# First attention of a two-layer network: one program over head pairs and halves of the queries, instead of two programs over whole head pairs

## The reference, cut to what matters

```
xn = layernorm(x, ln_scale, ln_bias)          # x: (2, 1024, 128), itself a layernorm of the input
q, k, v = (xn @ w) as (2, 16 heads, 1024, 8)  # for wq, wk, wv
probs = softmax(q @ k.T / sqrt(128))          # (2, 16, 1024, 1024)
out = probs @ v, heads side by side, + xn
```

## Time and profile before

| what | us |
|---|---|
| median of 3 runs | 1138.79 (1138.75 to 1138.86) |
| profiled execution | 1138.22 |
| its span, first to last instruction | 1136.4 |
| PE busy | 1016.6 |
| DVE busy | 730.4 |
| ACT busy | 664.9 |
| POOL busy | 395.1 |

### The profile page before, as it was taken

The page is one execution under the profiler, slowest core; times in us unless marked ns, Lnnn a source line. Parts: engine busy times, 40 slices in busy tenths (PEclk is TensorE's granted clock), DMA queues, the critical chain, the costliest instruction groups (busy, mean ns, idle before and its releaser), DMA issues. The chain is left out here.

```text
span 1136.4 us, 17320 instructions
## 1 busy us (share of the span) xinstructions
PE 1016.6 (89%) x5320; PEld 550.2 (48%) x5320; DVE 730.4 (64%) x1231; ACT 664.9 (59%) x1419; POOL 395.1 (35%) x340
## 2 busy tenths in 40 slices
PE   4499999999999997679579999999999999589997
PEld 3123333333333321423457676767777676456665
DVE  5588888888888870622744545545455554678997
ACT  4037777777777776312255655555565554357887
POOL 5650000000000000000567657493765730256665
PEclk9579999999999999589789999999999999789999
DMA  4300000000000000100000000000000000000001
GB/s 161 114 3 16 16 23 21 14 14 14 21 21 14 14 2 0 26 1 0 14 1 10 1 1 5 10 1 6 10 1 1 6 1 1 12 8 19 14 18 44
DMA packets 21230, 19.32 MB, mean 17 GB/s; under 512 B 5300, under 2 KB 15516, under 8 KB 21172
## 3 DMA queue, kind: packets, MB, share of 16 engines
q1 hardware_dynamic: 19844, 14.92, 4.5%
q0 software_dynamic: 528, 2.10, 0.5%
q10 hardware_dynamic: 800, 1.57, 0.4%
HBM read 14.26 MB, written 4.19 MB: 16 GB/s over the span
## 5 line engine op out<-in xcount | busy, mean ns | idle before, releaser
L484 ACT ACTIVATE probs<-score_bank 128x512 f32<-128x512 f32 x512 | 277.7, 594 | 121.4 <-PE score_bank L538 120.1
L415 DVE TENSOR_REDUCE maxima<-max_bank 128x1 f32<-128x1024 f32 x256 | 301.7, 1220 | 57.2 <-PE max_bank L505 55.2
L538 PE MATMUL score_bank<-q_stack,k_stack 100*128 100x512 bf16 x512 | 164.4, 387 | 7.0 <-ACT probs L484 5.0
L1105 ACT ACTIVATE a_probs<-a_scores,a_lowest 128x896 f32<-128x896 f32 (+7 forms) x128 | 94.9, 741 | 112.7 <-DVE a_lowest L1100 112.1
L505 PE MATMUL max_bank<-k_stack,q_stack 96*128 96x512 bf16 x512 | 143.9, 401 | 17.5 <-PEq L164 12.0
L1350 PE MATMUL a_sum<-a_turned,a_v 128*128 128x512 f32 (+3 forms) x384 | 158.5, 500 | 0.8 <-ACT a_headsT L1279 0.6
L549 PE MATMUL summed<-probs,v_tile 128*32 128x512 f32 x1024 | 136.4, 605 | 1.0 <-ACT probs L484 1.0
L709 POOL MEMSET m_padded<- 128x96 f32 x1 | 0.2, 178 | 383.6 <-POOLq L361 383.6
L1100 DVE TENSOR_REDUCE a_lowest<-a_scores 128x1 f32<-128x896 f32 (+7 forms) x128 | 96.2, 756 | 40.8 <-PE a_scores L1094 40.3
L538 PEld LDWEIGHTS score_bank<-q_stack,k_stack 100*128 100x128 bf16 x512 | 44.1, 97 | 157.2 <-ACT probs L484 143.1
L1482 POOL TENSOR_TENSOR m_gated<-m_linear,m_sigm 128x512 f32<-128x512 f32 x64 | 87.8, 1372 | 46.5 <-ACT m_sigm L1577 46.5
(11 more groups left out here) (220 smaller groups left out, 1583.4 us busy)
## 6 DMA issues: line engine op xcount, KB each, us to landing
rope<-in_rope POOLq DMA_DIRECT2D x1, 2048.0 KB, 11.9
m_w<-in_L_ffn_mlp_w SPq DMA_DIRECT2D x32, 64.0 KB, 1.8
q_stack<-q_parts SPq DMA_DIRECT2D x32, 48.0 KB
k_stack<-k_parts SPq DMA_DIRECT2D x32, 48.0 KB
q_stack<-q_parts SPq DMA_DIRECT2D x32, 32.0 KB
k_stack<-k_parts SPq DMA_DIRECT2D x32, 32.0 KB
out<-x SPq DMA_DIRECT2D x4, 256.0 KB, 2.4
q_parts<-l_q_parts SPq DMA_DIRECT2D x1, 768.0 KB, 3.5
```

Of the source, the lines that this page charges most:

```text
L415: dve.reduce_max(maxima[:, (s + away) % 2, n:n + 1], max_bank[n % 2][:, :], AX_X).then_inc(max_ready, 1)
L484: act.activation(probs[:, k % PROB_STEPS, j, :], score_bank[j % 2][:, :], ACT.Exp, scale=SCALE0).then_inc(prob_ready, 1)
L538: pe.matmul(score_bank[j % 2][:, :], k_stack[s % STACKS][x][rows, k * P:(k + 1) * P], q_stack[s % STACKS][rows, half * CH:(half + 1) * CH] ...
L1105: act.activation(probs[:, k % 2, c, 0:row_width(n)], scores[n % 2][:, 0:row_width(n)], ACT.Exp, bias=lowest[:, n % 8:n % 8 + 1], accum_out ...
```

## The change

One function, `layer0`, replaces both programs, with no barrier between projection and attention. Its work is in 32 units, each a head pair with half of the queries (512). A unit has eight steps of 128 keys.

- **Scores** lie in two halves of the rows: the first head in rows 0 to 49, the second in rows 64 to 113, of one k stack and one q stack (48 rows of products, 2 rows for the maxima). Each score matmul names its half (`tile_position=(x * ROW, 0)`). There are three score banks instead of two. Two scores a step.
- **Searches** contract all 128 rows, against a k stack that holds one head alone (`k_alone`), zeros elsewhere. One search a step; eight per unit; 256 in all. 12 of them are made ahead of the first score.
- **Ring**: the two double banks are now shared in strict turn by searches, the turned maxima (`turn`, at step 4) and the folded heads (`fold`, at step 6). PE may fill place p only when DVE has freed place p - 2.
- **Use** takes two steps of keys at once: four matmuls in four column strips, at steps 1, 3, 5 and 7. The four strips of `summed` hold two heads x two keys' parities; `fold`, four f32 matmuls of 18 columns, turns them and adds the two parities. It replaces the four transposes; DVE divides 64 instead of 128 results per row at a time, twice as often.
- **Start**: x comes in two halves, each normalised by itself. The first pair's parts are sent by themselves to DRAM and loaded from there in six DMAs. Loads of a later pair are 18 DMAs instead of 12. `rope` (2 MB, for the second layer) is loaded by SP during unit 0 instead of by POOL at the start. POOL instead of DVE stages the values.

The diff, cut to its core:

```diff
+ROW = 64
+VW = 32
+UNITS0 = B * H0
+TILES = TB
+LEAD = TILES + 4
+FOLD_AT = 6
+RING = 2
+SCORES = 3
+PROBS = 4
+VALUE = HD0 + 1
+def ring_of_step(u, k):
+    m = TILES * u + k + LEAD
+    if m < TILES * UNITS0:
+        yield "search", m
+    if k == LEAD - TILES and u + 1 < UNITS0:
+        yield "turn", u + 1
+    if k == FOLD_AT and u >= 1:
+        yield "fold", u - 1
...
+                    for part in range(3):
+                        rows = slice(first, first + (3 - part) * HD0)
+                        first += (3 - part) * HD0
+                        sp.dma_start(q_stack[stack][rows, :],
+                                     t.parts_dram[0][part, head, :].unsqueeze(0).broadcast_to([3 - part, HD0, S])).then_inc(loaded[stack], 16)
+                        for keys in (k_alone[stack][x], k_stack[stack]):
+                            sp.dma_start(keys[rows, :], t.parts_dram[1][0:3 - part, head, :]).then_inc(loaded[stack], 16)
...
+                def subtract(u):
+                    pair, half = divmod(u, 2)
+                    sp.wait_ge(freed, PLACE["turn", u] + 1)
+                    for part in range(2):
+                        row = NST + part
+                        sp.dma_start(q_stack[pair % STACKS][row:row + ROW + 1:ROW, half * CH:(half + 1) * CH],
+                                     shift[:, u % 2, part, :]).then_inc(shift_in[u % 2], 16)
...
+                send_first(0)
+                send_first(1)
+                sp.wait_ge(first_out, 16 * 6)
+                load_first()
+                send_parts(0)
...
+                for x in range(2):
+                    load_head(1, x)
+                send_parts(1)
+                subtract(0)
+                for u in range(UNITS0):
+                    if u + 1 < UNITS0:
...
+                    pair, x = u // 2 + 2, u % 2
+                    if pair < NPAIR:
+                        if pair >= STACKS:
+                            sp.wait_ge(score_ready, (pair - STACKS + 1) * 2 * 2 * TB)
+                        if pair == NPAIR // B and x == 0:
+                            sp.wait_ge(parts_out[1], 16 * 2)
+                        load_head(pair, x)
+                    if u == 0:
+                        sp.dma_start(t.rope[:, :, :], d["rope"].rearrange("a p s -> p a s")).then_inc(rope_in, 16)
...
+                    queries = slice(side * CH + qt * P, side * CH + (qt + 1) * P)
+                    for half in range(2):
+                        last = pe.matmul(max_bank[place % RING][:, half, :], q_stack[stack][:, queries],
+                                         k_alone[stack][x][:, half * CH:(half + 1) * CH], start=True, stop=True)
...
+                    for c in range(4):
+                        last = pe.matmul(max_bank[place % RING][:, 0, c * 2 * VALUE:(c + 1) * 2 * VALUE], heads[u % 2][:, c * P:(c + 1) * P],
+                                         fold[:, :, :].rearrange("p x w -> p (x w)"), start=True, stop=True)
+                    last.then_inc(filled, 1)
...
+                def give_ring(use):
+                    what, n = use
+                    place = PLACE[use]
+                    if place >= RING:
+                        pe.wait_ge(freed, place - RING + 1)
...
+                def score(u, k, x):
+                    pair, half = divmod(u, 2)
+                    rows, e = slice(x * ROW, x * ROW + NST + 2), 2 * (u * TB + k) + x
...
+                    if e >= SCORES:
+                        pe.wait_ge(prob_ready, e - SCORES + 1)
+                    pe.matmul(score_bank[e % SCORES][:, :], k_stack[pair % STACKS][rows, k * P:(k + 1) * P],
+                              q_stack[pair % STACKS][rows, half * CH:(half + 1) * CH], start=True, stop=True,
+                              tile_position=(x * ROW, 0)).then_inc(score_ready, 1)
...
+                    for slot in range(4):
+                        k, x = 2 * g + slot // 2, slot % 2
+                        last = pe.matmul(summed[VW * slot:VW * (slot + 1), :], v_tile[pair % 2][:, x, k, :], probs[:, k % PROBS, x, :],
+                                         start=(g == 0), stop=(g == GROUPS - 1), tile_position=(0, VW * slot))
+                    last.then_inc(used, 1)
...
+                        for x in range(2):
+                            score(u, k, x)
+                        for event in ring_of_step(u, k):
+                            give_ring(event)
+                        if k == 1 and u >= 1:
+                            use(u - 1, GROUPS - 1)
+                        if k % 2 == 1 and k >= 3:
+                            use(u, (k - 3) // 2)
+                use(UNITS0 - 1, GROUPS - 1)
+                give_ring(("fold", UNITS0 - 1))
...
-                def body(g, s):
-                    for k in range(TB):
-                        tiles = [tile for tile in searched_at(k) if ahead(g, s, tile[0])]
-                        for j in range(2):
-                            score(g, s, k, j)
-                        if first(g, s) and k == 0:
-                            search(g, s, *tiles.pop(0))
-                        if k > 0:
-                            use(g, s, k - 1)
-                        elif not first(g, s):
-                            use(g, s - 1, TB - 1)
-                        if k == 2 and not first(g, s):
-                            turn_heads(g, s - 1)
-                        if k == TURN_AT and ahead(g, s, 1):
-                            turn_maxima(g, s + 1)
-                        for j in range(2, 4):
-                            score(g, s, k, j)
-                        for tile in tiles:
-                            search(g, s, *tile)
```

More of the change, by code:

```diff
@@ L30 @@
 NST = 6 * HD0
-SHIFTS = 2 * NST
-VW = 32
 H1, KV1, D1 = 8, 4, 128
@@ L115 @@
 STACKS = 4
[L118 to L129, removed]
@@ L308, in layer0_attention, with ring_before, ring_uses, layer0 @@
+def ring_before():
+    for m in range(LEAD):
+        yield "search", m
+        if m == TILES:
+            yield "turn", 0
+def ring_uses():
+    yield from ring_before()
+    for u in range(UNITS0):
+        for k in range(TB):
+            yield from ring_of_step(u, k)
+    yield "fold", UNITS0 - 1
+PLACE = {use: i for i, use in enumerate(ring_uses())}
+def layer0(nc, t, d):
     ctx = ExitStack()
@@ L350, in ahead, with loads_by @@
-        def ahead(g, s, n):
-            return not isinstance(g, int) or 4 * g + s + n < NPAIR
-        def first(g, s):
-            return isinstance(g, int) and 4 * g + s == 0
-        def searched_at(k):
-            return [divmod(MAX_LEAD + 2 * k + i, TILES) for i in range(2)]
+        heads_ready, inverse_ready = sem("heads_ready"), sem("inverse_ready")
+        NW = 8
+        CB = NCH // B
+        GROUPS = TB // 2
+        LOADS = [6] + [18] * (NPAIR - 1)
+        SET = 4 * STACKS
+        def loads_by(pair):
+            return 16 * sum(LOADS[p] for p in range(pair % STACKS, pair + 1, STACKS))
@@ new lines, in normalise_chunk, with take_rest @@
+                def normalise_chunk(c):
+                    for tile in range(4 * c, 4 * c + 4):
+                        last = dve.tensor_scalar(normed[:, tile, :], t.x[:, tile, :], moments.both[:, tile, 0:1],
+                                                 moments.inverse[:, tile:tile + 1], ALU.subtract, ALU.mult)
+                    last.then_inc(normed_ready, 1)
+                def take_rest(i):
+                    which, c, cols = unit(i)
+                    dve.wait_ge(hi_ready, i + 1)
+                    if i >= 4:
+                        dve.wait_ge(lo_ready, i - 3)
+                    dve.tensor_tensor(rest[:, i % 4, :], bank_of_unit(i), parts[which][:, 0, cols], ALU.subtract).then_inc(rest_ready, 1)
@@ new lines, in take_ring @@
+                def take_ring(use):
+                    what, n = use
+                    if what == "search":
+                        search(n, PLACE[use])
+                    if what == "turn":
+                        split(n, PLACE[use])
+                    if what == "fold":
+                        divide(n, PLACE[use])
+                find(0)
+                normalise_chunk(0)
+                normalise_chunk(1)
+                find(1)
+                take_rest(0)
+                take_rest(1)
@@ L491, in _ @@
+                take(UNITS0 - 1)
             @block.tensor
             def _(pe):
[L493 to L507 removed]
```

597 lines of the change are left out of this document (284 added, 313 removed).

## The result

| | before | changed |
|---|---|---|
| median of the runs, us | 1138.82 (4 runs) | 1177.14 (1173.26 to 1180.12, 4 runs) |
| span of the profiled execution, us | 1136.4 | 1176.0 |
| first score of the first attention | 69.27 | 58.00 |
| end of its last division | 454.87 | 493.83 |
| from there to the end | 681.5 | 682.2 |

The changed kernel is slower: ratio 1.0335, interval 1.0308 to 1.0363. The forecast was 1167 us, in a range of 1136 to 1190. The attention starts 11.3 us earlier and takes 50.2 us longer from first score to end (435.8 against 385.6); what lies behind it is the same within 0.7.

A forecast was written before the change was run, and what follows sets the result against it. PE, without gaps, bound the kernel before; afterwards the two-place ring would hold PE. 1138.2 - 17.8 (start) + 45.7 (attention, units of 13.45) = 1166.1, median 1167 us, range 1136 to 1190.

The forecast's parts named there:

- the ring: Two shared bank places: PE waits for DVE's maxima at steps 4 to 5 and 6 to 7, 1.86 us each.
- 1.85, 1.86, 1.86, 1.05 and 1.28: Us between search starts: odd to even steps (four times), 4 to 5, 6 to 7, 0 to 1, 2 to 3.
- The sum 13.45: One unit of the middle in us, all eight search intervals added; 1.5 more than half of an old pair.
- Halves overlap: A step's two scores, in different row halves, take the price of one: 0.22 us, other bound 0.44.
- changes of form cost 0.10: Each new change of PE's array division between scores, search and use group costs 0.10 us, bounds 0 and 0.2.
- Serial halves: Rival: row halves do not overlap, a score pair costs 0.44, a unit 14.1 us, total 1187; chance 0.16.
- free changes: Rival: changing the array's division costs nothing, a unit takes 12.45 us, total 1137, not slower; chance 0.15.
- changes of 0.2: Rival: each change costs 0.2 us, twelve or so per unit, 14.4 or more, total above 1190; chance 0.08.
- From first score to end: First attention, first score to last division: 431.3 us against 385.6 before, +45.7, with 2 for half clock at the start.
- The start: Time until the first score: 51.5 us (49 to 56) against 69.27 before, a gain of 17.8.
- The first search: Searches begin at 35 us against 41.68: 5 less with rope moved and x halved, six loads at 1.1 each.
- half a pair: Old kernel's 11.93 us, the mark for one new unit; rival: a unit costs no more, 1121 us or less, chance 0.11.

The follow-up runs named there:

- Experiment 1: Changed kernel with the turned maxima placed ahead of step 4's search instead of behind it, for PE and DVE: 1152.33 us.
- experiment 6: Changed kernel with turned maxima and fold each ahead of their step's search, and the first maxima sent earlier: 1141.28 us, ratio 1.0024 to the kernel before.
- experiment 7: Changed kernel plus strings of score halves, searches and use groups behind the first attention, alternating and each kind alone, waiting for nothing: 1261.73 us, one run.
- Experiment 4: Changed kernel with SP sending the first maxima ahead of the second head's loads and the second sequence's parts: 1169.04 us, 8.1 less than the changed kernel.
- experiment 9: Kernel before with one edit: the rope table loaded during the first attention instead of at the start: 1138.08 us, ratio 0.9991.
- experiment 2: Changed kernel with each score matmul over all 128 rows instead of row halves, leaving out the separation of heads: 1174.63 us, 2.5 less than the changed kernel.
- experiment 3: Changed kernel with the use group ahead of the search in odd steps and the turn ahead of step 5's search: 1167.94 us, ratio 1.0248 to the kernel before.

## Why the prediction was right, and where it was off

- **What decides** was named rightly: the ring. Experiment 1 shows it by 24.8 us, and experiment 6 by some 29 of the 50.2 us by which the attention is longer; the other 20 are the changes of form, the fold and ACT, which the sum had too. The intervals forecast as 1.85, 1.86, 1.86, 1.05 and 1.28 came as 1.85, 1.92, 1.93, 1.14 and 1.27. The sum 13.45 was short by 0.23, thirty times 0.23 is 6.9 us. The terms that were too small are the two waits for DVE's maximum (1.86 for 1.92 and 1.93) and the one for ACT's exponential (1.05 for 1.14). For a maximum the sum had 1.18, half of the row for two; one by itself ends after 1.23 (243.30), and 0.64 + 1.23 + 0.05 is the 1.92. Of the signs named, one did not come: PE is busy 91.7% of the middle and not below nine tenths.
- **Halves overlap, changes of form cost 0.10**: both as forecast, by experiment 7. Serial halves, free changes and changes of 0.2 are out. The rule in the Trainium skill's "TensorEngine Tiling (Array Packing)", Key Properties, that a change of mode drains TensorE, agrees with the 0.10 to 0.12 us that each change costs here. The Trainium skill's "TensorE: Matmul & The Clock Gate", Measured speedup vs the span model, has 3.07 times for four row tiles; the estimate of 0.25 for two halves that the prediction worked out from it is a little dear: they take 0.22.
- **From first score to end**: 431.3 forecast, 435.8 measured: 6.9 more in the units, 1.6 less at the beginning (the first unit, whose first five us run at half clock, is 0.4 longer than the others, where 2 was allowed for the clock), 0.8 less in the tail.
- **The start** is the larger miss: first score 58.00 for 51.5, outside my 49 to 56. The mis-sized terms stand in SP's stream. From the end of the first loads until the parts were sent and landed it took 7.6 (32.9 to 40.48) and not 4.5; the eighteen loads took 10.7 (until 51.2) and not 11.7; the parts held SP 2.4 for 0.8; and from the issue of the maxima to the first score it was 4.4 instead of the 2.7 of the earlier trace rows, behind 1.5 MB of parts. Experiment 4 takes the last two away and gives 8.1 us.
- **The first search** came at 36.70 for 35, and so near by luck in part. The last part left at 24.8 and not at 22, so the gain there was 2 us and not 5, and the six loads took 4.7 and not 6.6. The reason with rope was wrong: by experiment 9 its 2 MB held the weights up but not PE, which waited for DVE.
- Together: 6.5 for the start, 4.5 for the attention and 0.7 behind it on the sum of 1166.1 make 1177.8; the profiled execution took 1178.45, the median is 1177.14. Both errors go the same way, and the median lies 10 us above the 1167, just outside the 1153 to 1176 that the forecast had for itself, and inside the stated range.

**Where half a pair's time went.** In experiment 6, where DVE holds almost nothing up, a unit is four double steps of 2.72 (two pairs of halves 0.44, two searches 0.87, a use group 0.87, five changes 0.54), the fold 0.91 (250.80 to 251.72), the turn with its short wait 0.26, and 0.27 and 0.41 at steps 1 and 3, where a score's bank waits for ACT: 12.73, measured 12.72. Half a pair before is four steps of 2.88 and 0.4: 11.93. So the halves save 1.76 us a unit (eight pairs at 0.22), and three more changes in a double step take back 1.3 of it; some 0.2 of small waits in before's four steps are gone; fold and turn cost 0.8 more, ACT's banks 0.7. Together that is 0.8 more than half a pair. On top of it the changed kernel has 0.96 of waits for the ring. The split of the 0.8 is worked out from rows; no run took the fold or ACT's waits away by themselves.

## What to carry to other kernels

- Count how often TensorE changes its form in a loop before splitting its rows or columns. Two halves at the price of one save 0.22 here, and a pair that stands between two whole-row matmuls gives it all back in two changes (experiment 2). By the prices of experiment 7 it pays to gather matmuls of one form first; no run here did.
- In a ring of two that one engine fills in order and another frees, a short task given behind a long one makes the filler wait for the long one. Give the short task first: 0.8 us a unit here, for two lines. But look at where the work moves: experiment 3, which also gave the turn first, put three tasks between two searches and gained 9 us, not 25.
- Time a large change in parts: here a start by which, alone, the attention ends 5.7 us earlier was hidden under a middle that takes 50 us longer.

## What the runs showed of the hardware that I had not expected

TensorE stood at half clock behind two short waits. In experiment 7, at the attention's end, it was busy 8.61 of 10 us; then it waited 0.81 us for ACT and 0.56 for DVE, with eight short matmuls between. Up to 492.0 the granted clock was 1.00, and from 492.5 on 0.50. The string, which waits for nothing, ran at 1.2 GHz until 498.7 and at 2.4 from there on (start:end, length, busy us per engine, granted clock, DMA):

```profile
480.00:490.00 10.00, 8.61 (x61) 2.60 (x61) 0.43 (x2) 8.21 (x16) 0.00 (x0) 1.00 0.00 0
490.00:492.70 2.70, 1.34 (x12) 0.97 (x8) 0.43 (x2) 0.60 (x1) 0.00 (x0) 0.89 0.00 0
492.70:498.70 6.00, 5.65 (x15) 0.95 (x16) 0.00 (x0) 0.00 (x0) 0.00 (x0) 0.50 0.00 0
498.70:509.00 10.30, 10.14 (x48) 2.52 (x48) 0.00 (x0) 0.00 (x0) 0.00 (x0) 0.99 0.01 2
```

And a change of form costs nearly the same at either clock, as far as the one pair of forms shows that ran at both. At half clock a round of halves and search takes 1.50 to 1.51 (494.23 to 495.73, 495.73 to 497.24). Twice the 0.22 and 0.44 is 1.32, which leaves 0.19 for two changes, as at full clock (0.20).
